# A build-time scheduler of a mixed graph and expert kernel: its list rule weighs step kinds by a table of preferences

## What is computed

```python
x = x + _L0_gnn_ref(_layernorm(x), adj, ...)      # and _L0_ffn_ref, _L1_gnn_ref, _L1_ffn_ref
...
x = x + _L2_gnn_ref(_layernorm(x), adj, ...)      # x + relu(conv(adj, layer_norm(x)))
x = x + _L2_ffn_ref(_layernorm(x), ...)           # a shared expert, and 2 of 8 routed ones, gelu, hidden 512
x = x + _L3_gnn_ref(_layernorm(x), nodemask, adj, ...)   # attention over the tile, times adj
x = x + _L3_ffn_ref(_layernorm(x), ...)           # 2 of 8 routed experts, relu, hidden 512
```

## Time and profile before

| | us |
|---|---|
| median of 3 runs (lowest, highest) | 3918.83 (3909.36, 3920.38) |
| the profiled execution | 3906.96 |
| its span | 3905.2 |
| PE busy, share of the span | 2542.3 (65%) |
| DVE | 2508.8 (64%) |
| ACT | 1311.6 (34%) |
| POOL | 1510.8 (39%) |

### The profile page before, as it was taken

The page is one execution under the profiler, slowest core; times in us unless marked ns, Lnnn a source line. Parts: engine busy times, 40 slices in busy tenths (PEclk is TensorE's granted clock), DMA queues, the critical chain, the costliest instruction groups (busy, mean ns, idle before and its releaser), DMA issues. The chain is left out here.

```text
span 3905.2 us, 44243 instructions
## 1 busy us (share of the span) xinstructions
PE 2542.3 (65%) x13000; PEld 1831.0 (47%) x13000; DVE 2508.8 (64%) x5200; ACT 1311.6 (34%) x2903; POOL 1510.8 (39%) x1358
## 2 busy tenths in 40 slices
PE   4789888888888888920000000067898888988981
PEld 2445555554455455510000000056787887877981
DVE  5898998889998885862433532677764344677112
ACT  3344445554454444410000000022333454443540
POOL 0010010000000017771677777113132747676576
PEclk8799999998899888965555555588898999988996
DMA  2000000000000041111000000023343666675873
GB/s 99 8 21 20 20 20 20 20 17 17 15 11 23 20 63 42 45 21 52 6 8 8 7 8 8 25 92 99 111 120 84 191 170 178 176 176 153 230 213 88
DMA packets 314156, 263.99 MB, mean 68 GB/s; under 512 B 102347, under 2 KB 247735, under 8 KB 313384
## 3 DMA queue, kind: packets, MB, share of 16 engines
q1 hardware_dynamic: 274824, 212.78, 19.3%
q0 software_dynamic: 39072, 48.21, 6.5%
HBM read 201.31 MB, written 60.82 MB: 67 GB/s over the span
## 5 line engine op out<-in xcount | busy, mean ns | idle before, releaser
L771 POOL TENSOR_TENSOR a_rstd<-a_var,minus_half 128x4 f32<-128x4 f32 x64 | 126.1, 1971 | 1293.0 <-DVE a_var L1305 1285.8
L1399 DVE TENSOR_TENSOR room<-room 128x1024 f32<-128x1024 f32 (+1 forms) x460 | 589.4, 1307 | 20.1 <-ACT room L1171 8.0
L364 PE MATMUL bank<-ident,room 128*128 128x128 f32 x192 | 29.9, 298 | 851.4 <-DMA room<-in_adj 811.1
L101 POOL DMA_INDIRECT gathered<-table_dram,slot_row x426 | 446.2, 1047 | 134.7 <-issue 134.7
L1941 POOL DMA_INDIRECT c_slots<-sent,c_tokens_of_slots x340 | 346.3, 1019 | 276.4 <-PE bank L2094 189.4
L364 PEld LDWEIGHTS bank<-ident,room 128*128 128x128 f32 x192 | 24.5, 153 | 855.6 <-DMA room<-in_adj 812.3
L1977 PE MATMUL bank<-c_expert_w,weights_f 128*128 128x128 f32 x2720 | 348.9, 285 | 21.6 <-DVE c_made L2339 20.7
L1977 PEld LDWEIGHTS bank<-c_expert_w,weights_f 128*128 128x128 f32 x2720 | 342.7, 201 | 30.4 <-issue 20.8
L1977 PE MATMUL bank<-c_slots_t,c_expert_w 128*128 128x256 f32 x1360 | 345.5, 400 | 5.3 <-ACT weights_f L2159 4.2
L2159 ACT ACTIVATE weights_f<-bank,c_expert_b 128x256 f32<-128x256 f32 x680 | 278.7, 471 | 202.9 <-PE bank L1977 202.8
L1403 DVE TENSOR_TENSOR room<-room 128x1024 f32<-128x1024 f32 x264 | 316.1, 1235 | 5.0
(11 more groups left out here) (492 smaller groups left out, 5521.4 us busy)
## 6 DMA issues: line engine op xcount, KB each, us to landing
c_expert_w<-in_weights_c SPq DMA_DIRECT2D x340, 256.0 KB
made<-c_made SPq DMA_DIRECT2D x170, 128.0 KB
results_dram<-a_results SPq DMA_DIRECT2D x64, 256.0 KB, 2.1
room<-results_dram SPq DMA_DIRECT2D x16, 1024.0 KB, 7.6
c_expert_b<-in_f_b SPq DMA_DIRECT2D x170, 64.0 KB
room<-in_adj SPq DMA_DIRECT2D x32, 256.0 KB, 5.4
sent<-c_rows_to_send SPq DMA_DIRECT2D x32, 256.0 KB, 2.4
gathered<-table_dram,slot_row POOLq DMA_INDIRECT x426, 2.4
```

The lines of the kernel that those rows point to most:

```text
L101: pool.indirect_dma_start(out=dst, out_offset=None, in_=env.table_dram, in_offset=bass.IndirectOffsetOnAxis(ap=index, axis=0), bounds_chec ...
L364: ins = nc.tensor.transpose(bank[0:n, j * P:(j + 1) * P], src[:, j, 0:n], ident[:, :])
L771: rstd.did(g_.tensor_tensor(st.rstd[:, :], st.var[:, :], env.minus_half[:, 0:GT], ALU.pow), what, k)
L1399: ins = v.tensor_tensor(dv[:, :, j, :], sv[:, :, 0, :], sv[:, :, 1, :], (ALU.min, ALU.max)[j])
```

## The change

The scheduler gets a table of preferences in us. A step is now chosen by the time at which it could start less its kind's preference: with a positive one it is taken although it could start up to that much later than others, with a negative one others are taken first. The time booked for it is the one at which it could start, as before. Nothing else changes: the same steps, the same buffers, the same waits.

```diff
+SOONER = {
+    "sum": -2.0, "leave": -1.0, "fetch": 5.0, "mark": -2.0, "f2_xt": 1.0, "load2": -8.0, "mask": -2.0, "load3": -1.0, "back": -2.0, "list": 0.5,
+    "conv": 0.5, "store": 1.0, "enter": -2.0, "agg": 0.5, "lift": -4.0}
...
             at = max([free[LONG["raise" if name in raises else name][0][0]]] + [done[w] + 0.1 for w in wants])
-            if best is None or (at, place) < best[:2]:
-                best = (at, place, name, k)
+            key = at - SOONER.get(name, 0.0)
+            if best is None or (key, place) < best[:2]:
+                best = (key, place, name, k, at)
         if best is None:
             break
-        at, place, name, k = best
+        _, place, name, k, at = best
```

## The result

The changed kernel takes 3881.74 us (median of 4 runs, 3876.9 to 3884.08) where the old one takes 3919.61 (4 runs, 3909.36 to 3921.7): ratio 0.9907, 95% interval 0.9887 to 0.9927, 37.9 us less by the medians. A later comparison on another chip gave 3879.5 where the old kernel took 3913.26, ratio 0.992 (0.9906 to 0.9933). The forecast was 63 us less, 3855.8; the range began at 3828 and ended at 3900. It is faster, by six tenths of what I worked out.

What follows compares the result with a forecast made beforehand. TensorE is full in quiet stretches, so only its idle time and clock can change, ahead of a GpSimd-bound tail. Gains 55 + 22 less 14 make 63 us, 3918.83 to 3855.8; range 3828 to 3900.

Steps and rivals of the forecast that it cites:

- (1): Routings two to six: matmuls now stand between the token marks; less TensorE idle time and slowness gain 55 us.
- (3): Gathers moved forward between routings: gains of 10 us at 3061, 7 at 3240 and 5 at 3471, sum 22.
- slowness 24: TensorE's half-speed steps: 19 us of the gain in routings two to six, 7 from moved gathers, less 2 for norm waits.
- lift 6: A norm now behind 36 DMAs on GpSimd: VectorE waits 8 us, TensorE 7 and is slow for 1.8; 9 lost.
- The sum of 39 without slowness: The whole kernel's gain with TensorE's half-speed steps left out: 39 us instead of 63.
- (4): Cost of moving gathers forward: norms wait behind GpSimd's DMAs and a weight load stands later; 14 us lost.
- Lift 5, ease 2 and ease 3 by the same queueing: 3: Three further norms held behind DMAs in GpSimd's queue: 3 us lost together.
- (2): First routing: enter 2 now stands behind list and pulls; gain 0, bounds -5 and +5 us.
- (5): Last layer's tail: GpSimd full with the same 94 DMAs, end a fixed 206 us behind; gain nothing, 8 if TensorE-bound.
- Half of it: Rival: marks interleave, but waits for routes and new norm waits take half the gain back; 3887 us, chance 0.18.
- GpSimd's queue: Rival: norms behind DMAs hold VectorE, and VectorE TensorE, making the kernel slower; 3946 us with ten such waits, chance 0.08.
- TensorE idle over 60 us outside the routings: Sign named beforehand that would show the forecast wrong: more than 60 us of TensorE idleness outside the routings.

Runs made afterwards that it cites:

- Experiment 1: Change cut to its preference for the marks: ratio to old kernel 0.9968 (slow chip), 0.9959 (quick chip); change without that preference: 1.0008 and 1.0009 (slow chips).
- Experiment 4: Old kernel plus 8 idle matmuls ahead of each token mark's wait but a routing's first, routings two to six: 3911.86 us against 3913.26, ratio 0.9995.
- experiment 3: Changed kernel, GpSimd issuing gathers after the next norm where their user stands behind it: 3940.21 us against the change's 3879.5 (quick chip); slow chip, ratio to old 1.0001.
- experiment 5: Norms' inverse deviation on VectorE by reciprocal, root left out, without GpSimd: old kernel so edited 4080.57 us, changed kernel 4050.17, unedited old 4103.69 (slow chip).

## Why the prediction was right in sign and too large

- **(1), idle time in the routings: right.** 42.9 us for 40.5 forecast and 76.4 before, each routing within 1.1 of its number. Waits for the marks are 23.3, a little over the 20 under which I wanted them. Experiment 1 shows the marks to be a part that gains by itself, 15.6 of the 33.8 us on the quick chip.
- **(1) and (3), slowness 24: wrong, and at least half of the miss.** TensorE's excess over the shortest steps fell from 82.8 to 77.1 (80.7 in the second trace), 2 to 6 us. Around the five routings, from the routing's own matmuls to the fifth step behind the last mark, it did fall, from 29.8 to 14.6 (18.1), 12 to 15 where 19 was forecast; but elsewhere it rose by some 10. The gatherings' own part fell from 9.6 to 0.3, but inside VectorE's 2.94 it had cost nothing. Of other steps that were over 0.8 us longer than their shortest there were 32 with 46.3 us before, and 30 with 41.8 (33 with 45.8) after: the half speed moved from behind the marks to behind lift 6 (lower 30), the first pull, the norms of layer 3. Beyond lift 6's 2 the sum had no term for slow steps behind waits that are new. Experiment 4 took the slowness away from the marks and gained 1.4.
- **The sum of 39 without slowness** was given beside the rule of the Trainium skill ("TensorE: Matmul & The Clock Gate", "Part 1: The HAM clock gate"). The medians then showed 37.9, but that is luck: in the traces 22 to 27 us are idle time and 2 to 6 slowness. Nor does the trace bear out the rule's size for this kernel: steps with a granted clock under 0.95 hold 70.5 us of the old kernel's excess and 63.1 of the new one's, 1.8 and 1.6% of the span in the last stage alone, not under 1%.
- **(4), norms behind GpSimd's DMAs: right mechanism, too small.** Lift 6 is as forecast (VectorE waits 9.30 for 8, TensorE 6.81 for 7). The term that was mis-sized is "Lift 5, ease 2 and ease 3 by the same queueing: 3", together with (3), which moved gathers forward in layer 3 at no price. Ease 5 and blend 14 stand behind gathers there, 5.30 and 4.02 on TensorE (nothing and 1.83 before) with half speed behind them, and they weren't in the sum. Norm waits rose by 13.7 to 16.1; experiment 3 shows that such waits reach TensorE, most of them directly, and experiment 5 is on the same side.
- **(4), load 6: 2, with bounds of 0 to 3.** Adj 13 waits 3.28 for its data (2.72 in the second trace), and the raise behind it is 1.7 slower: over the upper bound.
- **(2), first routing 0 (-5 to +5): -3.4 and -4.3**, with a pull's wait of 8.7 where 6 was forecast.
- **(3), 3061: right**, no wait at layer 3's first lower. **At 3471 it failed:** 5 were to be gained where the old kernel waits 4.07 for blend 10's norm, and the changed kernel still waits 3.02 there (3.21 in the second trace), with four steps behind that are 1.5 to 1.7 too long where the old one has one. 3240 gave 7 in the forecast. With the fourth and the fifth routing the two have 6.9 for 14.2 and -0.7 to 3.5 for 15.7.
- **(5), the tail: right**, 207.3 for 206.
- **The rivals.** "Half of it" (3887, chance 0.18) is nearer to what came than my own case, and its reason holds in part: the routes' first parts wait 4.4 us longer and norms that TensorE waits for directly 6.2, but slowness is the larger share of what is missing. GpSimd's queue did not make the kernel slower, but the same mechanism did in experiment 3. A part of that rival was priced too low: a busy VectorE lengthens GpSimd's issues, and I gave it 4 us. The last stage's 596 issues together took 608.3 us before and 620.2 after, 12 more, and in the fifth routing's stretch (3374 to 3409) thirteen issues of gathers average 1.19 us (number | busy us, mean ns of one | idle before):

```profile
L1960 POOL DMA_INDIRECT c_got<-made,c_places x13 | 15.5, 1192 | 4.0 <-issue 4.0
```

The Trainium skill ("SBUF — State Buffer", "Who interferes with whom") has some VectorE instructions shut GpSimd out for their whole length; the traces show longer issues, not which instruction caused them. How much of the 12 us reached TensorE no run tells.
- **The signs.** "TensorE idle over 60 us outside the routings" was no test: outside the five it idles 122 us, but the old kernel does so for 110. Nor does the range's upper end add up: (4) without its norm waits leaves 2, and 77 - 2 + 5 + 8 is 88, not 91.

## What to carry to other kernels

A queue that computes small things for others (here GpSimd's 56 inverse deviations) between long rows of DMA issues prices every reordering: count each issue moved ahead of such a step, and also ahead of the one after it, since when the queue is full a step helped is the next step harmed. When idle time is taken from one engine, don't add its half-speed steps to the gain; here they lay in a pace that another engine sets, or reappeared behind the next wait. And compare small changes on the chip on which they were profiled, or run the unedited kernel beside them each time: one chip's stalls hid a 0.7% loss.

## What the runs showed of the hardware

Of the three chips of the experiments two ran this kernel 4.9% slower (4103.15 and 4103.69 for 3913.26), with stalls on TensorE, ScalarE, VectorE and GpSimd for which the profile names no releaser, up to 21.9 us long in the last stage, and next to none on the third. An indirect DMA's issue on GpSimd takes 1.00 us while VectorE idles, and averaged 1.14 to 1.19 in the changed kernel's fifth routing, where VectorE is busy 30.6 of 35 us. TensorE's granted clock stayed at 1.00 through a stretch of marks with 16.08 us of 21 busy, and was 0.65 with 8.46 of 21; the step behind took 1.94 and 3.73.
